# Attention over 3125 nodes: turned blocks dealt anew to the seven steps, and which engine moves them out of PSUM

## The reference, cut to what matters

```
q, k, v = h @ Wq[head], h @ Wk[head], h @ Wv[head]
e     = leaky_relu(sum(q[src] * k[dst]), 0.2)            # one number per edge and head
ex    = exp(e - max of e over the edges into dst)
alpha = ex / max(sum of ex over the edges into dst, 1e-9)
out[dst] += alpha * v[src]                                # then x = x + out
```

## Time and profile before

| what | value |
| --- | --- |
| median of 3 runs | 2792.77 us (2784.33 to 2798.03) |
| profiled execution, span from first to last instruction | 2789.0 us |
| PE, DVE, ACT, POOL busy over the span | 82%, 65%, 52%, 68% |
| attention, first score product to last addition to X | 848.6 to 1753.9 us |

### The profile page before, as it was taken

The page is one execution under the profiler, slowest core; times in us unless marked ns, Lnnn a source line. Parts: engine busy times, 40 slices in busy tenths (PEclk is TensorE's granted clock), DMA queues, the critical chain, the costliest instruction groups (busy, mean ns, idle before and its releaser), DMA issues. The chain is left out here.

```text
span 2789.0 us, 65350 instructions
## 1 busy us (share of the span) xinstructions
PE 2275.2 (82%) x23024; PEld 1658.8 (59%) x23024; DVE 1811.8 (65%) x3137; ACT 1459.7 (52%) x2773; POOL 1889.4 (68%) x1286
## 2 busy tenths in 40 slices
PE   4577777774974888888888888778997999999998
PEld 3466666662432555555656566533544788888887
DVE  8799999994344776777777776411113666666665
ACT  0498989983025888888888887100002333223222
POOL 3487878831506877777787775277775787888884
PEclk7699999996985999999999999899997999999999
DMA  2366767666803111111111112898693332222223
GB/s 52 113 178 189 193 193 196 188 187 186 206 23 88 50 49 49 49 49 49 49 49 49 49 49 16 185 220 189 123 219 72 72 61 59 58 60 56 60 53 60
DMA packets 241964, 285.30 MB, mean 102 GB/s; under 512 B 162714, under 2 KB 180451, under 8 KB 238566
## 3 DMA queue, kind: packets, MB, share of 16 engines
q1 hardware_dynamic: 193035, 248.38, 36.0%
q0 software_dynamic: 48784, 35.00, 6.6%
HBM read 170.23 MB, written 112.10 MB: 101 GB/s over the span
## 5 line engine op out<-in xcount | busy, mean ns | idle before, releaser
L384 POOL DMA_INDIRECT scratch_slots<-sort_pay,sort_slot x440 | 638.8, 1452 | 201.3 <-issue 200.3
L1908 POOL TENSOR_TENSOR score<-score,rise 125x1000 f32<-125x1000 f32 x261 | 559.2, 2162 | 234.3 <-DVE peaks L1850 193.5
L2283 POOL DMA_INDIRECT gathered_rows<-scratch_projected,src_i x385 | 474.0, 1231 | 125.4 <-issue 116.8
L1850 DVE CUSTOM_DVE_ANT_0 score<-raw,log_in 125x1000 f32<-125x1000 f32 (+1 forms) x348 | 330.4, 969 | 177.4 <-PE raw L1707 104.5
L1727 PE MATMUL probsT<-ident,score 125*125 125x125 f32 x2175 | 352.2, 292 | 25.8 <-ACT score L1784 14.8
L1774 ACT ACTIVATE rise<-raw 125x1000 f32<-125x1000 f32 (+1 forms) x350 | 312.7, 918 | 114.0 <-PE raw L1707 75.9
L1727 PEld LDWEIGHTS probsT<-ident,score 125*125 125x125 f32 x2175 | 293.1, 198 | 104.4 <-DVE weighed L1864 56.7
L861 PE MATMUL built<-pair_weight,hot 125*128 125x125 bf16 x3750 | 247.1, 227 | 86.4 <-DVE pair_weight L806 85.1
L861 PEld LDWEIGHTS built<-pair_weight,hot 125*128 125x128 bf16 x3750 | 225.2, 103 | 103.4 <-DVE pair_weight L806 102.1
L1707 PE MATMUL raw<-QT,key 32*125 32x500 f32 x1200 | 182.7, 678 | 93.9 <-DVE peaks L1850 88.4
L1864 DVE COPY weighed<-probsT 125x500 f32<-125x500 f32 x400 | 250.0, 671 | 13.2 <-PE probsT L1727 12.7
(11 more groups left out here) (305 smaller groups left out, 4341.2 us busy)
## 6 DMA issues: line engine op xcount, KB each, us to landing
weights_in<-scratch_weightsT SPq DMA_DIRECT2D x50, 1093.8 KB
scratch_weightsT<-wT SPq DMA_DIRECT2D x25, 1367.2 KB
scratch_logs<-log SPq DMA_DIRECT2D x75, 437.5 KB
log_in<-scratch_logs SPq DMA_DIRECT2D x75, 437.5 KB
counts_in<-scratch_counts SPq DMA_DIRECT2D x25, 683.6 KB
scratch_counts<-cc SPq DMA_DIRECT2D x24, 683.6 KB
scratch_slots<-sort_pay,sort_slot POOLq DMA_INDIRECT x440
weights_in<-scratch_weightsT SPq DMA_DIRECT2D x50, 127.0 KB
```

The lines of the kernel that those rows point to most:

```text
L384: nc.gpsimd.indirect_dma_start(rows, bass.IndirectOffsetOnAxis(ap=slot[:, c:c + 1], axis=0), pay[:, c, :], None).then_inc(sort["placed"][u ...
L1850: nc.vector.tensor_tensor_reduce(out=halves(score[u][h]), in0=seen, in1=halves(log_in[:]), scale=1.0, scalar=FLOOR, op0=ALU.add, op1=ALU.m ...
L1908: nc.gpsimd.tensor_tensor(score[u][h][:, here], score[u][h][:, here], rise[:, b, PIECE * (1 - k):PIECE * (2 - k)], ALU.add).then_inc(added, 1)
L2283: nc.gpsimd.indirect_dma_start(gathered[:, g % GATHERS, k, :], None, projected, bass.IndirectOffsetOnAxis(ap=src_i[:, FIRST + g, k:k + 1], ...
```

## The change

New tables deal turns and sums to the steps apart from each other. Turns 8 to 23 of block t-2 go four to a step into g0 to g3, turn 24 with turns 0, 1 and 2 of block t-1 into g4, 3 to 5 into g5, 6 and 7 into g6. PE does all turns of a step first and all its sums after them. `turn_mixed` and `finish` go to g6, `turn_mixed` between turns 6 and 7; the mixed values take the bank after turn 6's, so from a = 7 on every turn's place in the ring of banks shifts by one. ACT moves four score blocks (0, 4, 5 and 7) and DVE twenty-one, still after both log passes; DVE's `finish` comes after them. In g0 ACT's first `rise` pass waits for one of POOL's additions of g5 and the second for both, and in g5 POOL does its two additions in the other order.

```
+    TURNS_OLD = ((8, 9, 10, 11), (12, 13, 14, 15), (16, 17, 18, 19), (20, 21, 22, 23), (24,), (), ())
+    TURNS_NEW = ((), (), (), (), (0, 1, 2), (3, 4, 5), (6, 7))
+    SUMS_OLD = ((3, 4, 5, 6, 7), (8, 9, 10, 11, 12), (13, 14, 15), (16, 17, 18, 19, 20), (21, 22, 23, 24), (), ())
+    SUMS_NEW = ((), (), (), (), (), (0, 1, 2), ())
+    MIX_STEP = LAST
+    MIX_AFTER = 6
+    COPY_STEP = 4
+    SWAPPED = LAST - 1
-    BY_ACT = (0, 2, 3, 4, 6, 7, 8, 10, 11)
+    BY_ACT = (0, 4, 5, 7)
...
+        bank_turn = lambda a: a if a <= MIX_AFTER else a + 1
+        mixed = probsT[:, (MIX_AFTER + 1) % 3, 0:D]
+        def blocks(old, new, t, u, g):
+            return ([(t - 2, u, a) for a in old[g] if has(t - 2)] + [(t - 1, 1 - u, a) for a in new[g] if has(t - 1)])
...
+            def wait_bank(t, place):
+                if place == MIX_AFTER + 4:
+                    pe.wait_ge(finished, t + 1)
+                    wait_moved(pe, t, before_in_bank[place - 6])
+                elif place >= 3:
+                    wait_moved(pe, t, before_in_bank[place - 3])
+                elif not (known(t) and t == 0):
+                    wait_moved(pe, t - 1, (23, 24, 22)[place])
...
             def tile(t, u):                      # PE
                 for g in range(GROUPS):
                     if has(t):
                         score_group(t, u, g)
+                    turns = blocks(TURNS_OLD, TURNS_NEW, t, u, g)
+                    for of, of_u, a in turns:
+                        if a <= MIX_AFTER or g != MIX_STEP:
+                            turn_probs(of, of_u, a)
+                    if g == MIX_STEP and has(t - 2):
+                        turn_mixed(t - 2)
+                    for of, of_u, a in turns:
+                        if a > MIX_AFTER and g == MIX_STEP:
+                            turn_probs(of, of_u, a)
+                    for of, _, a in blocks(SUMS_OLD, SUMS_NEW, t, u, g):
+                        sum_values(of, a)
...
             def tile(t, u):                      # DVE
                 for g in range(GROUPS):
-                    if g == LATE + 1 and has(t - 2):
-                        finish(t - 2, u)
                     if has(t):
                         add_logs(t, u, g)
+                    for of, of_u, a in blocks(TURNS_OLD, TURNS_NEW, t, u, g):
                         if a not in BY_ACT:
                             move_probs(of, of_u, a)
+                    if g == MIX_STEP and has(t - 2):
+                        finish(t - 2, u)
...
                 for half in range(2):            # ACT, raise_group
+                    if not (known(t) and t == 0 and g < 2):
+                        if g == 0:
+                            act.wait_ge(added, t * (2 * GROUPS) + (half - 3))
+                        elif half == 0:
+                            act.wait_ge(added, t * (2 * GROUPS) + 2 * (g - 1))
...
-                    for k, first in enumerate((2, 0)):     # POOL
-                        if k == 0:
+                    for at_once, (k, first) in enumerate(((0, 2), (1, 0)) if g != SWAPPED else ((1, 0), (0, 2))):
+                        if at_once == 0:
```

More of the change, by code:

```diff
@@ L1589, in attention @@
         mixedT = values_ps[:, 0:P]
-        mixed = probsT[:, 0, 0:D]
+        bank_turn = lambda a: a if a <= MIX_AFTER else a + 1
+        before_in_bank = {bank_turn(a): a for a in range(TILES)}
+        mixed = probsT[:, (MIX_AFTER + 1) % 3, 0:D]
         key_loaded = [sem(f"key_loaded{u}") for u in range(2)]
@@ L1718, in turn_probs @@
                     pe.wait_ge(exped, t * HEADS + HEADS)
[L1719 to L1725, removed]
+                place = bank_turn(a)
+                wait_bank(t, place)
                 for h in range(HEADS):
-                    ins = nc.tensor.transpose(probsT[:, b, h * P:(h + 1) * P], score[u][h][:, a * P:(a + 1) * P],
+                    ins = nc.tensor.transpose(probsT[:, place % 3, h * P:(h + 1) * P], score[u][h][:, a * P:(a + 1) * P],
                                               ident[0:P, 0:P])
@@ L1732, in sum_values @@
                 wait_moved(pe, t, a)
+                if a == 0 and not (known(t) and t == 0):
+                    pe.wait_ge(mix_copied, t * 1)
                 for h in range(HEADS):
@@ L1739, in turn_mixed @@
                 if has(t + 1):
-                    wait_moved(pe, t + 1, 3)
+                    wait_bank(t + 1, MIX_AFTER + 1)
                 pe.wait_ge(mix_copied, t + 1)
@@ L1745, in tile @@
                 for g in range(GROUPS):
-                    if g == LATE + 1 and has(t - 2):
-                        turn_mixed(t - 2)
                     if has(t):
                         score_group(t, u, g)
[L1750 to L1758, removed]
+                    turns = blocks(TURNS_OLD, TURNS_NEW, t, u, g)
[9 more added lines that the diff above has]
+                        sum_values(of, a)
             pe.sem_inc(mix_turned, 1)
@@ L1767, in raise_group @@
                 act.wait_ge(scored, t * GROUPS + (g + 1))
-                if not (known(t) and t == 0 and g < 2):
-                    act.wait_ge(added, t * (2 * GROUPS) + 2 * (g - 1))
                 n = PW if g < LAST else TAIL
                 for half in range(2):
+                    if not (known(t) and t == 0 and g < 2):
[3 more added lines that the diff above has]
+                            act.wait_ge(added, t * (2 * GROUPS) + 2 * (g - 1))
                     if half == 1:
@@ L1797, in move_probs @@
                 wait_slot(act, t, a)
-                nc.scalar.copy(weighed[:, a % RING].rearrange("p h d -> p (h d)"), probsT[:, a % 3, 0:PW]).then_inc(moved_act, 1)
+                nc.scalar.copy(weighed[:, a % RING].rearrange("p h d -> p (h d)"), probsT[:, bank_turn(a) % 3, 0:PW]).then_inc(moved_act, 1)
             def copy_mixed(t):
@@ L1810, in tile @@
                             steepen(t, u)
[L1811 to L1816, removed]
+                    for of, of_u, a in blocks(TURNS_OLD, TURNS_NEW, t, u, g):
+                        if a in BY_ACT:
+                            move_probs(of, of_u, a)
+                    if g == COPY_STEP and has(t - 2):
                         copy_mixed(t - 2)
@@ L1821, in tile @@
                         keep_positive(t - 1, 1 - u)
-                    for a in mine[1:]:
-                        move_probs(of, of_u, a)
             act.wait_ge(tiny_made, 1)
@@ L1863, in move_probs @@
                 wait_slot(dve, t, a)
-                nc.vector.tensor_copy(weighed[:, a % RING].rearrange("p h d -> p (h d)"), probsT[:, a % 3, 0:PW]).then_inc(moved_dve, 1)
+                nc.vector.tensor_copy(weighed[:, a % RING].rearrange("p h d -> p (h d)"), probsT[:, bank_turn(a) % 3, 0:PW]).then_inc(moved_dve, 1)
             def finish(t, u):
@@ L1878, in tile @@
                 for g in range(GROUPS):
-                    if g == LATE + 1 and has(t - 2):
-                        finish(t - 2, u)
                     if has(t):
                         add_logs(t, u, g)
-                    of, now = values_of(t, g)
-                    of_u = u if g < LATE else 1 - u
-                    for a in now:
+                    for of, of_u, a in blocks(TURNS_OLD, TURNS_NEW, t, u, g):
                         if a not in BY_ACT:
                             move_probs(of, of_u, a)
+                    if g == MIX_STEP and has(t - 2):
+                        finish(t - 2, u)
                     if g == LAST and has(t):
```

2 lines of the change are left out of this document (removed).

## The result

The changed kernel takes 2930.43 us, median of 4 runs (2924.83 to 2938.62), against 2791.68 (2784.33 to 2798.03) before: ratio 1.0498, 95% interval 1.0467 to 1.0528. It is **slower by 139 us, 5.0%**. The forecast was 2905, 113 us slower, in a range of 2830 to 2950. The profiled execution took 2938.62 us with a span of 2936.9.

A forecast was written before the change was run, and what follows sets the result against it. Waits between engines inside a step, with no engine full, were taken to bound attention. Steps and small terms, +46, plus clock falls, +67, gave +113 on the 2789.0 span, 2902; 3.8 for the median made 2905, range 2830 to 2950.

The forecast's parts named there:

- The steps at full clock: Steps g0 to g6 of an attention block, with five waits for DVE's move: 36.88 us against 33.82.
- the term of +47: Blocks 2 to 24 with the longer steps at full clock: 846.3 us against 798.9.
- The clock: PE's waits in g0 to g4 bring two clock falls a block at 1.45 us each: +67 us.
- The clock that stays up: Rival: the same longer steps in attention but no clock falls, 2839 us; chance 0.25.
- The wait that vanishes: Rival: the bank is free when PE reaches the fourth turn of g0 to g4, -143 us, 2650; chance 0.07.
- The clock that stays down: Rival: turns don't hold the clock up, every block might run at 1.2 GHz, 3230 us; chance 0.03.
- ACT's relief and DVE's load: Five moves a block pass from ACT to DVE: at most 3 us off ACT, 3 us onto DVE, costed at nothing.
- The swap on POOL: POOL's additions in g5: without the swap about 1 us a block would be due, with it nothing.
- Moves held back by sums: DVE's moves 9 and 14 wait for sums 3 and 8, end about 7.4 us after the product: free.
- Block 1: Has no turn 24, so no such wait, and shorter g5 and g6: -3 us.
- Tail: DVE moves 17 blocks at the end instead of 13: +2 us.

The follow-up runs named there:

- experiment 3: Changed kernel with one or two plain 500-column products on PE before the turn that precedes the waiting one: 2850.30 us.
- experiment 8: Kernel before the change, with turns 21 and 24, the last of g2 and g3, done three times: 2765.44 us, ratio 0.9914.
- experiment 5: Changed kernel with DVE's first move of g0 to g4 put between its two log passes: 2727.40 us, ratio 0.9769 to the kernel before.
- experiment 4: Changed kernel with sums whose blocks are already moved run ahead of the waiting turn in g0 to g4: 2750.27 us, ratio 0.9837 to the kernel before.
- experiment 7: Kernel before the change, with only ACT's moves cut to blocks 0, 4, 5 and 7: 2788.60 us against 2794.03.

## Why the prediction was right

**The steps at full clock were right to a tenth of a microsecond.** Forecast 6.38, 6.23, 5.73, 6.23, 6.51, 3.85, 1.95, together 36.88; measured in experiment 3, in odd blocks, 6.46, 6.18, 5.82, 6.18, 6.47, 3.86, 1.95, together 36.92. The 4.35 and 4.50 at which the fourth turn starts, taken from the earlier trace rows, are in the trace after as 4.41 in the block shown and 4.35 in experiment 3; g0's 4.50 came out as 4.63 in odd blocks.

**One piece of that sum was missed.** Even blocks take 37.35: g0 is 6.89. I had DVE free at 3.4 after g6's product and wanted at 3.5, "close, but free". DVE in block 8 of the changed kernel, whose product starts at 1157.74:

```profile
1158.98 0.18 DVE L1866 TENSOR_REDUCE shift<-peaks 125x4 f32<-125x32 f32 x1
1159.83 1.20 DVE L1858 CUSTOM_DVE_ANT_0 score<-raw,log_in 125x1000 f32<-125x1000 f32 x1 [0.67 <-PE probsT L1734]
```

The first pass starts 2.09 after the product, not 1.53, and 0.67 after `find_shift` has ended; in odd blocks it is 0.24 after it. The profile puts the 0.67 down to PE, but the loop body holds two blocks, and the trace has a compare-and-branch of DVE's sequencer in this gap, from 1159.03 to 1159.09, with its next instruction 0.25 us later. So it is in all ten blocks from 4 to 22 that begin with a jump back, with gaps of 0.66 to 0.70, and in none of the odd ones, with 0.24 or 0.25. In the kernel before, DVE's idle 2.62 hid it. It is worth 0.43 in every second block, and with the small differences above the term of +47 measured +52.5 (the 77.4 of experiment 8 less the 24.9 that the falls had cost before).

**The clock was the right mechanism and its size was low.** Forecast two falls a block at 1.45, +67; measured 57 falls, 2.5 a block, at 1.55, +88.6. This is most of the 25 us by which the forecast of 2905 is under the 2930 measured. Four tenths was the rate for a wait of 2.3 us in two pieces; single waits of 1.7 to 2.5 us in a row bring a fall in 57 of 115. The two pieces were not the right ones either: they were the 1.08 and the 1.24 us before g4 and in it, and experiment 8 shortens the 1.39 and the 1.08, leaves the 1.24 whole, and has no fall. My waits were also too short, 1.5 to 2.1 against 1.73 to 2.48 in the profile where the clock is full: I put three turns and their drain at 1.60 + 0.17, and twelve transposes in a row take 1.57 with it in the trace after, and g0 has its 0.43 in even blocks. The nearness that I argued from pointed the right way, and the rows of before had no case to size it by.

**Rivals.** The clock that stays up, 2839, is what experiment 3 shows when the waits are filled (2850), so its price was right and its condition was not met. The wait that vanishes and a faster kernel fell with the first row of the trace after; the point from which it decides, a fourth turn by 3.8 us, fits experiment 5, where 3.4 makes the kernel faster than before. It counts the sums behind the turn; in experiment 4, with the sums ahead, a turn at 4.47 will do. Its working has 4 x 0.63 behind the waits and needs five of them for its 9.2. The clock that stays down didn't come, and the low stretches ended after 3.5 us on average. Of the Trainium skill's page "TensorE: Matmul & The Clock Gate", the section "A second HAM failure mode: psum-queue depth-cycling", by which short idles between groups of matmuls make the clock swing, agrees with the 57 stretches here. Its section "Part 4: PE-mode transpose", by which turns don't count for the clock, is contradicted again by experiment 8, where nothing but turns was added and every fall went.

**Small terms.** ACT's relief and DVE's load were costed at nothing; experiment 7 has them at 0.12 us a block. The swap on POOL was said to keep 1 us a block away; on the kernel of experiment 5 it keeps 0.4 without the falls and 0.6 with them. Moves held back by sums were costed at nothing; DVE has 76 such waits for a slot, 75 us, and the steps at full clock came out without a term for them. Block 1: -2.4 for -3. Tail: +0.8 for +2.

## What to carry to other kernels

When work is dealt out evenly over steps, look at what each piece needs from its own step. With three banks the fourth turn of a step waits for the step's first move, wherever that stands on its engine; put the move early, and what is ready ahead of the wait, before you count any engine's load. And where PE waits as long as here, 1.7 to 2.5 us several times a block, count the waits twice: once for themselves, and once for the clock that falls behind them. Waits of at most 1.5 us brought none in experiments 4 and 5, though the 1.39 and 1.08 close together in the kernel before did.

## What was not expected of the hardware

A loop body of PE that grew by 44 transposes a block made the instruction queue carry 182 packets instead of 90 and cost 3.7 to 4.6 us at each of ten jumps back; with 24 more a block it was 108 packets and two stalls, of 6.0 and 6.3 us. The jump back at the end of DVE's loop shows as 0.43 us in g0 once DVE has no idle time there. Work whose result is thrown away made two kernels faster: 80 us in experiment 3, 29 in experiment 8.
